# Laying out the q, k and blank rows of an attention stage in reading order, and moving its maxima, preparation and first loads

## The reference

```python
# L0_attn: layernorm, projection, causal conv, state-space recurrence, gate, output projection; added to x
# L0_ffn:
nx  = layernorm(x)
q, k, v = split(nx @ Wqkv + bqkv)                    # 16 heads of 8 features
scores  = where(causal, q @ k.T / sqrt(8), lowest)   # per head, 2048 x 2048
attn    = softmax(scores)
x1  = (attn @ v) @ Wo + bo                           # then a mixture of 8 experts, top 2
# L1_attn: a second state-space layer; L1_ffn: a gated network with ternary weights
```

## Time and profile before

| | |
|---|---|
| median of 3 runs | 1386.39 us (1384.39 to 1389.28) |
| profiled execution, its own time | 1388.94 us |
| its span, first to last instruction | 1387.2 us |
| busy: PE, DVE, ACT, POOL | 1184.4, 902.4, 783.0, 292.5 us |
| mixer, up to the first exponential of attention | 254.3 us |
| attention, 16 items | 522.4 us |
| the rest | 610.6 us |

### The profile page before, as it was taken

One profiled execution on the slowest core, in us unless ns is written; L12 is line 12 of the kernel. 1 busy time (PEld: TensorE's weight loads), 2 busy tenths in 40 slices (PEclk: granted clock), 3 DMA queues, 4 the chain that ended last, 5 costly groups with the idle time before them and its releaser, 6 DMA issues.

```text
span 1387.2 us, 15933 instructions
## 1 busy us (share of the span) xinstructions
PE 1184.4 (85%) x5716; PEld 599.6 (43%) x5776; DVE 902.4 (65%) x1684; ACT 783.0 (56%) x1135; POOL 292.5 (21%) x208
## 2 busy tenths in 40 slices
PE   4668876778989998889999999999886968679998
PEld 2444543433333333333323466565432424237776
DVE  4576866797898788888853453444377686983443
ACT  3667843444544555556678654456686566425554
POOL 3223344100000000000001100000096666850000
PEclk9779998999999999999999999999988889889999
DMA  2222266425000000000000222211131212200000
GB/s 90 62 61 62 53 117 106 83 47 107 9 1 2 1 1 1 1 1 0 1 17 17 74 64 71 73 45 39 76 107 66 80 71 74 84 15 0 8 8 16
DMA packets 52111, 62.98 MB, mean 45 GB/s; under 512 B 7864, under 2 KB 42304, under 8 KB 49984
## 3 DMA queue, kind: packets, MB, share of 16 engines
q1 hardware_dynamic: 52032, 61.95, 17.0%
HBM read 51.05 MB, written 4.46 MB: 40 GB/s over the span
## 4 chain that ended last, share of the span: by engine, by line
PE 52%; DVE 20%; ACT 10%; POOL 6%; issue 5%; DMA 1%; SPq 1%; another core or an unknown queue 0%; DVEq 0%; ACTq 0%; POOLq 0%
DVE mx L1142 9%; PE psum L1230 8%; PE psum L1513 7%; PE psum L1200 6%; PE psum L1130 6%; PE psum L388 5%; PE psum L390 5%; PE psum L389 5%; POOL drive L1953 3%; DVE hst L1971 3%; PE psum L1904 2%; ACT probs L1214 2%; ACT psum L1913 1%; DMA kz<-qk_part_rows 1%; PE psum L1203 1%
## 5 line engine op out<-in xcount | busy, mean ns | idle before, releaser
L1214 ACT ACTIVATE probs<-psum 128x1024 f32<-128x1024 f32 (+1 forms) x320 | 288.4, 938 | 207.4 <-PE psum L1200 106.4
L1142 DVE TENSOR_REDUCE mx<-psum 128x1 f32<-128x512 f32 (+3 forms) x640 | 345.3, 602 | 66.1 <-PE psum L1130 48.4
L1130 PE MATMUL psum<-kz,qa 128*128 128x512 bf16 (+3 forms) x620 | 186.7, 353 | 43.7 <-DVE mx L1142 26.1
L1200 PE MATMUL psum<-qa,kz 128*128 128x512 bf16 (+1 forms) x600 | 175.8, 362 | 8.4 <-ACT probs L1214 3.0
L1904 PE MATMUL psum<-hst,ident 128*128 128x512 f32 x256 | 134.8, 672 | 39.3 <-DVE hst L1971 21.6
L1953 POOL TENSOR_TENSOR drive<-du,b_bc 128x1024 f32<-128x1024 f32 x64 | 149.5, 2355 | 24.8 <-DVE hst L1971 24.2
L1230 PE MATMUL psum<-probs,v 128*32 128x512 f32 (+3 forms) x1280 | 150.7, 543 | 0.3 <-ACT probs L1214 0.2
L1531 DVE TENSOR_TENSOR hid<-hid,gate_bc 128x1024 f32<-128x1024 f32 x64 | 78.8, 1241 | 109.0 <-ACT hid L1523 106.8
L1971 DVE TENSOR_TENSOR_SCAN hst<-psum,hlast,drive 128x512 f32<-128x512 f32 x96 | 115.7, 1263 | 33.6 <-ACT psum L1913 28.2
L1523 ACT ACTIVATE hid<-psum,cols 128x512 f32<-128x512 f32 x128 | 85.0, 688 | 76.1 <-PE psum L390 75.6
L1130 PEld LDWEIGHTS psum<-kz,qa 128*128 128x128 bf16 x640 | 60.9, 98 | 143.0 <-DVE mx L1142 85.4
(11 more groups left out here) (293 smaller groups left out, 1834.1 us busy)
## 6 DMA issues: line engine op xcount, KB each, us to landing
b_bc<-b_rows SPq DMA_DIRECT2D x16, 1024.0 KB, 4.7
cs_bc<-cs_rows SPq DMA_DIRECT2D x16, 512.0 KB, 6.8
gate_bc<-gate_rows SPq DMA_DIRECT2D x32, 256.0 KB, 3.2
ew_raw<-experts_dram SPq DMA_DIRECT2D x8, 512.0 KB, 3.6
qk_part_rows<-qk_parts SPq DMA_DIRECT2D x8, 384.0 KB, 2.7
qa<-qk_part_rows SPq DMA_DIRECT2D x48, 64.0 KB
kz<-qk_part_rows SPq DMA_DIRECT2D x96, 32.0 KB
fw_raw<-net_dram SPq DMA_DIRECT2D x11, 256.0 KB, 2.7
```

What stands on the lines that cost most here:

```text
L1130: ins = pe.matmul(out[:, 0:w], qa[:, b, h // 2, i * P:(i + 1) * P], kz[:, h // 8, c, h % 8, 0:w], start=True, stop=not last, skip_group_ch ...
L1142: dve.tensor_reduce(mx[:, 4 * i + h % 4, c:c + 1], fill_bank("mx", k, n)[:, 0:w], AX.X, ALU.max).then_inc(S["mx_read"], 1)
L1200: ins = pe.matmul(out[:, lo:], kz[:, h // 8, kt // TPB, h % 8, kt % TPB * P:(kt % TPB + 1) * P], qa[:, b, h // 2, lo:], start=True, stop=n ...
L1214: act.activation(probs[:, st % 2, hh, :, lo:], s_pair[n % 2][:, :, lo:], ACT.Exp, scale=SCALE).then_inc(S["p_done"], 1)
```

## The change

It has five parts. (1) **Layout.** `cs_rows`, `part_dram` and a new `blank_dram` lie in DRAM in the order in which they are read: one run of 4 KB (k, blank, cs) or 8 KB (q) for each partition in place of runs of 1 KB or 512 B. `kz` gets its even and odd heads apart for that. A block is stored by six DMAs, not two. (2) **Preparation.** Blocks 0 and 1 are prepared in the mixer with v one step later; block 2's matmuls move into items 0 and 1, block 3's into items 2 and 3. (3) **Maxima.** A table, made once, gives for each step and quarter the units made there. It spreads a cost of the units evenly over a cost of the steps and no longer in proportion to their number. (4) **Early maxima.** DVE takes three units of item 0 ahead of `yn` of block 3, and the mixer's PE list is regrouped. (5) **Start.** Only the first quarter of x is loaded ahead of the other inputs, and POOL waits for `xn` of block 0 before it makes `wk`.

```diff
-        part_dram = nc.dram_tensor("qk_part_rows", (2, 3, P, T), BF16, kind="Internal").ap()
+        part_dram = nc.dram_tensor("qk_part_rows", (2, NB, 3, 2, HDA, HA // 2, BLK), BF16, kind="Internal").ap()
+        blank_dram = nc.dram_tensor("blank_rows", (2, P, HA // 4 * BLK), BF16, kind="Internal").ap()
...
-        def unit_share(k, step):
-
-            steps = 2 * (ITEMS[k][0] + 1)
-            if k + 2 >= len(ITEMS):
-                return []
-            n = len(units(k + 2))
-            return list(range(n * step // steps, n * (step + 1) // steps))
+        def step_cost(b, kp):
+
+            return sum((BLK - max(0, kt - TPB * b) * P) / BLK for kt in (2 * kp, 2 * kp + 1)) / 2
+
+        def unit_cost(k, n):
+            b, _, i, c = units(k)[n]
+            return 0.2 + 0.8 * (1 if c < b else (i + 1) / TPB)
...
+        MX_LEAD = 2.5
+        def maxima_table():
...
+                due.append((min(max(starts[STEPS.index((k, 0))] - MX_LEAD, 0.4 * starts[STEPS.index((k, 0))]), starts[STEPS.index((14, 0))] + 1.0), done))
...
+                    quota = max([(total - spent) * dt_ / max(d - now, dt_) for d, total in left], default=0.0)
+                    due_at = max(due_at, spent) + quota
+                    while item < 16 and spent + unit_cost(item, n) / 2 <= due_at:
+                        table[s][hh].append((item, n))
...
             for j in range(2):
                 sp.wait_ge(S["parts_done"], 2 * b + j + 1)
-                sp.dma_start(part_dram[j][:, :, tt].rearrange("n p t -> p n t"), qk_parts[:, j, :, :]).then_inc(S["parts_saved"], 16)
+                for n in range(3):
+                    sp.dma_start(part_dram[j, b, n].rearrange("par e pair t -> pair par e t"), qk_parts[:, j, n, :]).then_inc(S["parts_saved"], 16)
...
             for par in range(2):
                 for g, n in enumerate(K_ROWS):
                     r0 = 64 * par + g * HDA
-                    src = part_dram[1, n].rearrange("(half pair par e) t -> par half e pair t", half=2, par=2, e=HDA)[par]
                     for half in range(2):
-                        sp.dma_start(kz[r0:r0 + HDA, half, b, par::2, :], src[half][:, :, tt]).then_inc(parts_loaded[b % 2], 16)
+                        sp.dma_start(kz[r0:r0 + HDA, half, b, par, :, :], part_dram[1, b, n, par, :, 4 * half:4 * half + 4]
+                                     ).then_inc(parts_loaded[b % 2], 16)
...
-            store_sp(sp, 2)
             mrow_sp(sp, 1)

             sp.wait_ge(S["x_mixed"], NB)
             blank_sp(sp, 2)
             mrow_sp(sp, 2)
+            store_sp(sp, 2)
             sp.wait_ge(parts_loaded[0], LOADS * 16)
             load_q_sp(sp, 2)
             mrow_sp(sp, 3)
...
-        PREP_PE = {(0, 1): 1, (1, 0): 2}
+        PREP_PE = {(0, 0): (2, "x"), (0, 1): (2, "q"), (1, 0): (2, "k"), (1, 1): (2, "v"),
+                   (2, 0): (3, "x"), (2, 1): (3, "q"), (3, 0): (3, "k"), (3, 1): (3, "v")}
...
-                        share = unit_share(k, step)
-                        for n in share[len(share) * hh // 4:len(share) * (hh + 1) // 4]:
-                            mx_pe(pe, k + 2, n)
+                        for item, n in MX_AT[step_base[k] + step][hh]:
+                            mx_pe(pe, item, n)
...
+            if b == NB - 1:
+                early_dve(o, dve, G)
             dve.wait_ge(S["y_rstd"], b + 1)
...
-            sp.dma_start(x_tok[:, :, :], a["x"].rearrange("b (i p) d -> p (b i) d", p=P)).then_inc(S["in_x"], 16)
+            sp.dma_start(x_tok[:, 0:TPB, :], x_rows[:, 0:TPB, :]).then_inc(S["in_x"], 16)
             sp.dma_start(cols[:, :], a["cols"]).then_inc(S["in_x"], 16)
             sp.dma_start(w_raw[:, :], a["win"]).then_inc(S["in_win"], 16)
+            sp.dma_start(x_tok[:, TPB:, :], x_rows[:, TPB:, :]).then_inc(S["in_rest"], 16)
...
             front_pool(o, pool, 0, 0)
+            pool.wait_ge(S["ln_xn"], 1)
             pool.wait_ge(S["in_win"], 16)
...
-            pe.wait_ge(S["qk_evac"], 2 * NB - 2)
-            pe.wait_ge(S["v_done"], NB - 1)
-            pe.wait_ge(S["mrow_done"], 4)
+            pe.wait_ge(S["qk_evac"], NB)
+            pe.wait_ge(S["v_done"], NB // 2)
+            pe.wait_ge(S["mx_read"], unit_base[2])
             attention_pe(pe)
```

More of the change, by code:

```diff
@@ L829, in build @@
+        MX_AT = maxima_table()
+        MROW_AT = {}
+        for s, quarters in enumerate(MX_AT):
+            for hh, quarter in enumerate(quarters):
+                for item, n in quarter:
+                    if n == len(units(item)) - 1:
+                        MROW_AT[divmod(4 * s + hh + 3, 4)] = item
         parts_loaded = [sem("parts_loaded_even"), sem("parts_loaded_odd")]
         def prep_bank(kind, b):
-            return fill_bank(kind, b) if b == NB - 1 else ring.bank(kind, b, 0)
+            return fill_bank(kind, b) if b >= LATE else ring.bank(kind, b, 0)
@@ L843, in prep_pe @@
                 pe.wait_ge(S["nx_ready"], b + 1)
-                for j, kind in enumerate(("pq", "pk")):
-                    out = prep_take(pe, kind, b)
-                    pe.matmul(out[:, :], wqkv_raw[:, j, :], nx[:, :], start=True, stop=True).then_inc(S["qk_filled"], 1)
+                out = prep_take(pe, "p" + part, b)
+                pe.matmul(out[:, :], wqkv_raw[:, "qk".index(part), :], nx[:, :], start=True, stop=True).then_inc(S["qk_filled"], 1)
+            elif part == "v":
                 out = prep_take(pe, "pv", b)
@@ L1129, in mx_pe @@
             last = c == b
-            ins = pe.matmul(out[:, 0:w], qa[:, b, h // 2, i * P:(i + 1) * P], kz[:, h // 8, c, h % 8, 0:w], start=True, stop=not last,
+            ins = pe.matmul(out[:, 0:w], qa[:, b, h // 2, i * P:(i + 1) * P], kz[:, h // 8, c, h % 2, h % 8 // 2, 0:w], start=True, stop=not last,
                             skip_group_check=True)
@@ L1344, in attention_dve @@
                 for step in range(2 * (ITEMS[k][0] + 1)):
-                    for n in unit_share(k, step):
-                        mx_dve(dve, k + 2, n)
-                    if step == 0 and 2 <= k + 1 < 16:
-                        mrow_dve(dve, k + 1)
+                    for hh in range(4):
+                        for item, n in MX_AT[step_base[k] + step][hh]:
+                            mx_dve(dve, item, n)
+                            if n == len(units(item)) - 1:
+                                mneg_dve(o, dve, item)
+                        if (step_base[k] + step, hh) in MROW_AT:
+                            mrow_dve(dve, MROW_AT[step_base[k] + step, hh])
                     if step == 1 and k >= 1:
@@ L2314, in _ @@
                     elif what == "prep":
-                        prep_act(act, b, n)
+                        for part in PREP_STEP_ACT[n]:
+                            prep_act(act, b, part)
                     else:
@@ L2377, in _ @@
                     elif what == "prep":
-                        prep_pe(pe, b, n)
+                        for part in PREP_STEP_PE[n]:
+                            prep_pe(pe, b, part)
                     else:
```

218 lines of the change are left out of this document (131 added, 87 removed).

## The result

The changed kernel takes 1391.53 us in the median of 20 runs, the kernel before 1386.7 in its 20: a ratio of 1.0046 (95% interval 1.0027 to 1.0065; the ratio is formed from all runs, the quotient of the two medians is 1.0035). It is slower by 0.3 to 0.65%, where 1382 was forecast. The profiled execution took 1393.08 us, 4.1 more than that of before; two more profiled executions took 1388.01 and 1397.73.

The account below looks back on a forecast made before the run. It took attention to be near PE's limit, with DVE close behind. Terms -6.4 - 9 + 5 + 6 = -4.4 took the profiled 1388.94 us to 1384.5, or 1382 as median against 1386.4; range 1362 to 1397, 8 in 10.

Parts of the forecast that it names:

- Start, -6.4: Kernel start: x no longer all ahead of `cols` saves 2 us, `xn` without POOL's `wk` beside it 4.5 more; ends -4 and -7.
- Transition, -9: Before attention: transposes of block 3 5.3 us earlier and a 4.0 us wait gone; ends -2 and -12.
- (a): Loads before attention: larger pieces move faster, so `kz` is there at 209 instead of 216.55.
- (c): Before attention: transposes L507 start at about 213 and not 218.3, 5.3 us earlier.
- The store's price, +1.5: Storing a block in six DMAs instead of two costs 1.5 us a block, ends 0 and 3.
- (b): Before attention: v of block 1 stands behind `yn`, so `yst` can be up to 3 us earlier.
- (d): Before attention: block 2's preparation leaves the chain, and with it PE's wait of 3.98 us.
- Items 0 to 3, +5: First attention items: SP's list brings item 3's maxima rows late, a stall of about 4 us; ends -5 and +14.
- Items 4 to 14, +6: Later attention items: step prices sum to +10.5, less 4.5 us because units are not alike; upper end +16, lower -18.
- C: Rival: loads to 8 partitions stay slow, bound by the partitions and not the piece; +5.6, median 1392; chance 0.20.
- B: Rival: maxima levelled as the weights want, PE becomes the bound in items 4 to 13; -28, median 1358; chance 0.22.
- D: Rival: attention dearer, last steps stay near 5 us and SP stalls items 3 and 4; +6.6, median 1393; chance 0.12.

Follow-up runs that it names:

- fast loads: Third layout, loads filling 48 partitions in place of 8, in the changed kernel with all five parts: ratio 0.9899 to before; without table and early maxima 0.9865.
- equal units: Changed kernel with the maxima units of item k+2 in equal numbers on the steps of item k, all else as changed: ratio 0.9950 to before.

## Why the prediction was wrong, point by point

The two profiled executions differ by 4.2 us of span, where the sum said -4.4. By the traces: start -2.0 (at the store of block 0), store to attention +6.5, items 0 to 3 +7.8, items 4 to 13 -3.3, items 14 and 15 +0.7, what follows -5.5.

- **Start, -6.4.** Right in both mechanisms at the start itself: `xn` 1.11 us, PE's first transposes at 8.24 in place of 16.66. Alone it is worth -9 by the medians (ratio 0.9935). But in the changed kernel only 1.3 to 2.9 us were left at the store of block 0. The term took the gain to pass through the mixer whole; part of it went where TensorE's granted clock fell (0.66 in 93 to 99 us, 0.50 in 135 to 141).
- **Transition, -9: the step that failed**, in (a). I took the cost of a piece to be the limit and 209 for `kz`; it came at 217.0, 212.0 and 217.5. The eight neighbouring partitions are the limit, 73 and 74 GB/s for 8 KB and 1 KB in one execution. With it fell (c): the maxima that need `kz` stand ahead of L507 in PE's list, and three of them now ahead of `yn` on DVE. And "nothing is added" for the first scores was wrong, they wait 10.3 us for the rows. I had read the earlier trace rows as if the rows of item 0 stood at 241.72 because of the loads; these had been issued by 238.9, and SP waited for `mrow`. With `mrow` earlier and the loads no shorter to issue, SP's list became the limit. From the store to attention it is 73.2, 64.6 and 72.9 us in place of 66.7 and 64.2: on average some 5 us later where I had 9 earlier. The store's price, +1.5, was 2.9 to 3.5 (loads begin 6.6 to 7.2 us after the store's issue and not 3.7). Steps (b) and (d) were sound: `yst` comes 20.0 us behind the store in place of 22.5, and with fast loads the changed kernel needs 57.9, or 56.8 without table and early maxima, so the 9 us are there.
- **Items 0 to 3, +5.** Measured +7.8; the place and the kind of the stall were right, 5.8 in place of 4 us. The inner split was not: items 0 and 1 take 40.7 us where I had 35.
- **Items 4 to 14, +6.** Against equal units in the same kernel, items 4 to 13 differ by 0.1 us and item 14 by 0.7: +1. Against the first profile of before they are even 3.3 and not more, but there two falls of the clock lie in them. The signs were right item by item; the gains in items 6 and 7 were larger (6.9 and 5.9 us against 4.8 each), the losses in 5, 8, 9 and 13 smaller (2.0, 4.6, 3.6 and 3.0 against 3.4, 5.4, 5.0 and 4.8). Last steps take 4.2 us as forecast. Full ones with 10 units take 6.9 and 7.2 where I had 7.16, and 9 take 6.15 where I had interpolated 6.5. The reductions in them are not shorter (5.63 and 5.77 us for 10, against 5.49 in the earlier trace rows), so the reason I gave, cheaper units, is not shown. The steps, answering to the earlier trace rows:

```profile
580.43:587.29 6.86, 5.63 (x10) 1.00 0.03 4
587.29:594.45 7.16, 5.77 (x10) 1.00 0.00 1
594.45:600.60 6.15, 5.17 (x9) 1.00 0.00 0
600.60:604.82 4.22, 2.40 (x4) 1.00 0.01 4
```

- **The rest, 0.** After attention the changed kernel was 5.5 us faster in the profile, and 605.0 to 607.2 in three profiles against 610.6 and 608.6, with the same work. Other versions of it took 604.9 to 609.0. This difference was not counted and is not explained.
- **The rivals.** C was right in its bound, the eight partitions. That its 1392 is the measured 1391.5 is partly luck: it had 2 us of gain in the transition and +6 for the table, where the traces show 6.5 of loss and about +1, and nothing for the lost start and the 5.5 us at the end. I gave C 0.20 since later loads had moved 102 GB/s with the same pieces. That row said little: the pace of such loads varies from 66 to 114 GB/s whatever the piece. B did not come: PE works 351.5 us of items 4 to 13 in 377.1. D was right only in the stall at item 3.
- **The range**, 1362 to 1397, held the time; the sign was wrong. I had given slower 0.32 and faster 0.46.

## What to carry to other kernels

Before a layout is changed for larger pieces, look which partitions a DMA fills: twelve loads to eight neighbours each are slow in any piece (66 to 114 GB/s here, against 174 for 48), and small DMAs issued behind them are late too. Where two paths end at the same wait, removing one shows nothing, so test both together. Work that is put ahead of a chain must not wait for something that the chain doesn't need, on any of the engines that the chain passes. And before a difference of a few us between two profiles is explained, take a second profile of each.

## What the hardware showed that I had not expected

- In one execution eight neighbouring partitions take in 73 and 74 GB/s (8 KB and 1 KB), eight that lie 4 apart 111, and 80 get 248. In other executions the same loads to eight neighbours run at 66 to 114.
- A store of the same bytes moves 231 to 272 GB/s when its DRAM side starts with 128 rows, and 163 or 164 when it starts with a dimension of 8, with the DMA share falling from 0.69 or more to 0.52.
- TensorE's granted clock took two courses through the same instructions (1.00, or 0.57 and 0.56 in the stretches above). The executions are 12 us apart, 6.3 us of it at the store of block 0.
